# Attention value products of a vision tower: one product for both heads of a step in place of one for each

## The chip, the cores and the metric

The kernel runs on one core of one Trainium2 chip. The metric is the device time of one execution, in microseconds (us). Five engines matter: PE (matrix products, with its weight loads PEld shown apart), ACT, DVE and POOL (elementwise work), and SP, which here only issues transfers. ACT and POOL issue transfers too.

## The reference

64 images become 196 patches and a class token each (197 tokens, 192 features). One causal self-attention layer with 12 heads of 16 features follows, then a layernorm, then a top-2 expert layer with 8 experts and a second layernorm.

```python
q, k, v = jnp.split(x @ w_attn + b_attn, 3, axis=-1)     # 12 heads of 16
att = jnp.einsum('bhqd,bhkd->bhqk', q, k) * (1.0 / math.sqrt(HS))
att = jax.nn.softmax(jnp.where(causal, att, -jnp.inf), axis=-1)
y = jnp.einsum('bhqk,bhkd->bhqd', att, v)
y = y.transpose(0, 2, 1, 3).reshape(Bx, Tx, Cx) @ w_proj + b_proj
```

The change touches the last einsum and how its result reaches the projection.

## The kernel before, in words

The attention part works on pairs of images (32 pairs) in a software pipeline of 36 bodies; each full body works on several pairs at once, in different stages. A body has 12 steps, and a step handles two heads (one pair `j` of heads) of one image. All engines run the same list of steps, and the order on each is written out by hand; the engines meet at semaphores only. Each engine takes its instructions in order, so an instruction that waits holds up all that follow it.

In step s, in this order:

- PE makes turned scores `ST` (keys on the rows) for the step 9 steps back (`turned_first` L634, `turned_second` L640), the scores `S` that give the row maxima (L646, L652, with masks at L658 and L659), and the value products for the step 11 steps back into the one bank `Y` (`values`, L668 and L672). Behind these stand the pieces of the table `PIECES`: `QK` (L589), `V` (L745 to L749), `PR`, the projection (L759), `MX`, the turning of maxima (L724), and the embedding `EB` (L601) of the next pair.
- ACT copies `Y` to `ysb` (L490) in every third step (2, 5, 8, 11), then takes the exponential of `ST` into `p32` (L495, L497), then in steps 0, 3, 6, 9 issues the transfer `rb <- rd` (L507), and then drains what the pieces made (`qk_hi` L521, `nm` L527 with a transfer of its own L531, `vp` and `hres` L545 and L549, `pay` L563, `x_hi` L466).
- DVE reduces `S` to maxima (L841, L844), in steps 2, 5, 8, 11 multiplies `y = ysb * rb` (L852) for the group before and then takes the reciprocal `rd` of the sums (L861), and drains pieces.
- POOL masks `p32` (L430, L434) and splits `x` (L412).

`ST` has one buffer: its next product waits for the exponential of the last. `Y` has one buffer: three steps (six heads) add up in it, and the first value product of a group waits for `ysb` of the group before (semaphore `s_yc`).

The layout of `Y` before: each head has 102 value columns in `vp`, 96 for the features of a group of six heads, zero but for its own 16, and six for the sums of probabilities, one of them ones. So each head's product goes to the same 102 rows and 198 query columns, and adds only to its own rows. A step needs four products: the first 128 keys (198 queries) and the last 70 keys (70 queries) of either head. `p32`, `vp` and `Y` are plain float32, and the compiler makes two PE instructions of each such product. The sums stand on rows 96 to 101 of `Y`; their reciprocals are spread over the 96 feature rows by the transfer `rb <- rd`.

```python
if opens: first_keys(*heads[0], True, False)
for hh, h in heads: last_keys(hh, h)
if not opens: first_keys(*heads[0], False, False)
first_keys(*heads[1], False, j % 3 == 2).then_inc(s_pv, 1)
```

Of the kernel before, what the change touches and what calls it, by code (L numbers as in the profile page):

```python
# [33 lines left out]
P = 128  # L34
# [35 lines left out]
VW1 = CH + NH // 2  # L70
KV = 2 * NH * VW1
# [129 lines left out]
def attention_block(nc, d, shared):  # L201
    with ExitStack() as ctx:
# [9 lines left out]
        wp, wpt = sb("wp", [CH + 1, 2, CX], F32), sb("wp_turned", [CH, 2, C], F32)  # L212
# [3 lines left out]
        bqk, bv = sb("bqk", [P, 3], F32), sb("bv", [CH, 2], F32)  # L216
        bvs = sb("bv_columns", [CH, 2, P], F32)
# [27 lines left out]
        rd, rb = sb("rd", [P, 2, TI], F32), sb("rb", [CH, 2, TI], F32)  # L245
        y = [sb(f"y{n}", [CH + 1, 2, TI], F32) for n in range(2)]
# [56 lines left out]
        def body_at(i):  # L303
            return Banks(i, stages_of(i) if isinstance(i, int) else ALL, full, drained)

# [152 lines left out]
        def _(act):  # L458
            act.dma_start(wp[0:CH, :, E:], d["wp"]).then_inc(s_w, 16)
# [19 lines left out]
            def body(i, turn, par, stages):  # L479
                g = body_at(i)  # L480
                for s in range(STEPS):
                    m = (i - 1) * STEPS + (s - LAG)
                    if s % 3 == 2 and is_step((i - 1) * STEPS + (s - 1) - LAG_PV):

                        im, j, back = value_step(s - 1)
                        grp = j // 3
                        u = (i - back) * 4 + (im * 2 + grp)
                        wait(act, s_ym, u - 1)
                        act.wait_ge(s_pv, (i - 1) * STEPS + (s - LAG_PV))
                        act.activation(ysb[0:VW1, grp, :], Y[0:VW1, 0:TI], ACT.Copy).then_inc(s_yc, 1)  # L490
# [23 lines left out]
                    for name in g.pieces(s):  # L514
# [18 lines left out]
                        elif name[0] == "V":  # L533
                            t = int(name[1])
                            im, hf, _, rows = TILES[t]
                            g.wait_full(act, name)
                            if t < 2:
                                wait(act, s_pv, (i - 2) * STEPS + 6)
                            else:
                                wait(act, s_pv, (i - 2) * STEPS + 12)  # L540
                            if isinstance(i, int) and i == 1:
                                act.wait_ge(s_vset, 4)
                            dst = bass.AP(vp[im], hf * NH * VW1,
                                          [[KV, rows], [6 * VW1, 2], [VW1 + HD, 6], [1, HD]])
                            act.activation(dst, src[0:rows, 0:C].rearrange("p (g h e) -> p g h e", g=2, h=6),  # L545
                                           ACT.Copy).then_inc(s_vc, 1)
# [38 lines left out]
        def _(pe):  # L585
# [30 lines left out]
            for h in range(2):  # L616
                for f in range(2):
                    mm = pe.matmul(G[1][0:CH, h * E:(h + 1) * E], wpt[:, f, h * CH:(h + 1) * CH], wgc[:, f, :],
                                   start=(f == 0), stop=(f == 1))
# [3 lines left out]
            for f in range(2):  # L623
                pe.matmul(G[1][:, 0:CX], bvs[:, f, :], wp[0:CH, f, :], start=(f == 0), stop=False)
# [36 lines left out]
            def values(im, j, b):  # L661

                heads = [(hh, 2 * j + hh) for hh in range(2)]
                opens = j % 3 == 0

                def first_keys(hh, h, start, stop):
                    v0 = vp[im][:, h * VW1:(h + 1) * VW1]
                    return pe.matmul(Y[0:VW1, 0:TI], v0, p32[b][:, hh, 0:TI], start=start, stop=stop)  # L668

                def last_keys(hh, h):  # L670
                    v1 = vp[im][0:T1, (NH + h) * VW1:(NH + h + 1) * VW1]
                    pe.matmul(Y[0:VW1, P:TI], v1, p32[b][0:T1, hh, TI:TI + T1], start=False, stop=False)  # L672

                if opens:
                    first_keys(*heads[0], True, False)
                for hh, h in heads:
                    last_keys(hh, h)
                if not opens:
                    first_keys(*heads[0], False, False)
                first_keys(*heads[1], False, j % 3 == 2).then_inc(s_pv, 1)  # L680

            def body(i, turn, par, stages):
                g = body_at(i)
                for s in range(STEPS):
# [23 lines left out]
                    if is_step(n - LAG_PV):  # L708
# [4 lines left out]
                        if j == 0:  # L713
                            pe.wait_ge(s_vset, 4)
                            pe.wait_ge(s_vc, (i - back) * 4 + (2 * im + 2))
                        pe.wait_ge(s_mask, m * 2 + 2)
                        values(im, j, (s + 1) % 3)
                    for name in g.pieces(s):
# [32 lines left out]
                        elif name[:2] == "PR":  # L751
# [3 lines left out]
                            for hf in range(2):  # L755
                                rows, col = T1 if hf else P, hf * P
                                for f in range(2):
                                    feat = slice(0, CH + 1 - f)
                                    mm = pe.matmul(G[b][0:rows, hf * CX:(hf + 1) * CX],  # L759
                                                   y[im][feat, f, col:col + rows], wp[feat, f, :],  # L760
                                                   start=(f == 0), stop=(f == 1))
# [18 lines left out]
        def _(dve):  # L780
# [11 lines left out]
            for n in range(2):  # L792
                dve.memset(y[n][CH:CH + 1, 0, :], 1.0).then_inc(s_qset, 1)
# [7 lines left out]
            dve.tensor_copy(bvs[:], bv[:].unsqueeze(2).broadcast_to([CH, 2, P])).then_inc(s_const, 1)  # L801
# [8 lines left out]
            dve.tensor_copy(wp[0:CH, :, 0:E], G[1][0:CH, 0:2 * E].rearrange("p (a b) -> p a b", a=2))\  # L810
# [6 lines left out]
            dve.tensor_tensor(wp[CH:CH + 1, 0, :], G[1][CH:CH + 1, 0:CX], bp[CH:CH + 1], ALU.add).then_inc(s_const, 1)  # L817
# [7 lines left out]
            def body(i, turn, par, stages):  # L825
# [4 lines left out]
                for s in range(STEPS):  # L830
# [16 lines left out]
                    if s % 3 == 2 and is_step(n - LAG_PV - 4):  # L847
# [3 lines left out]
                        dve.wait_ge(s_rb[grp], ((i - back) * 2 + (im + 1)) * 16)  # L851
                        dve.tensor_tensor(y[im][0:CH, grp, :], ysb[0:CH, grp, :], rb[:, grp, :],  # L852
                                          ALU.mult).then_inc(s_ym, 1)
                    if s % 3 == 2 and is_step(n - LAG_PV - 1):
# [6 lines left out]
                        dve.reciprocal(rd[CH:VW1, grp, :], ysb[CH:VW1, grp, :])\  # L861
# [117 lines left out]
                    if isinstance(i, int) and i == 0 and s == 6:  # L979
# [5 lines left out]
                        for n in range(2):  # L985
                            dve.memset(bass.AP(vp[n], CH, [[KV, P], [6 * VW1, 4], [VW1 + 1, 6]]), 1.0)\
                                .then_inc(s_vset, 1)
# [554 lines left out]
```

## Time and profile before

| | |
|---|---|
| median of 3 runs | 2326.57 us (2326.23 to 2331.97) |
| the profiled execution: its time | 2324.15 us |
| its span in the trace | 2322.4 us |
| TensorE clock granted, mean | 0.968 of full speed |
| busy over the span | PE 92%, PEld 89%, DVE 68%, POOL 68%, ACT 47% |
| instructions | 49007, of them PE 14772 |

The attention part fills the first 1,300 us or so, the expert part the rest. A row of a timeline gives the start in us, the duration, the engine, the line, the operation, the tile written, the tiles read and the shapes; in brackets stands how long the engine was idle before it and who released it. Matmuls overlap: the next one starts in the trace before the last one ends, so a product's price on PE is the distance from start to start. A row of ACTq is ACT's sequencer issuing a transfer.

### The profile page before, as it was taken

Reading aid. Unit: us, or ns where it says so; the run is one execution under the profiler, and the core shown is the slowest. Engines: PE = TensorE matmul, PEld = TensorE weight load, DVE = VectorE, ACT = ScalarE, POOL = GpSimd, SP = SyncE. Lnnn points to the kernel's source line nnn. Section 1 sums busy time; section 2 is a strip of 40 time slices with the busy share of each in tenths; the row PEclk is TensorE's granted clock in tenths of the full one; section 3 lists DMA queues with packets and bytes.
Section 4 is the critical chain, followed back from the end, with each engine's and each line's share of the span. In section 5 each row is a group of like instructions: output and inputs, shape, how many; then the busy total and the mean of one; then the engine's idle time right before and its main releaser. Section 6 shows DMA issues by size and latency. Waiting matters only on the chain. (4 is left out here: it accounts for less than half of the span.)

```text
span 2322.4 us, 49007 instructions
## 1 busy us (share of the span) xinstructions
PE 2134.6 (92%) x14772; PEld 2068.0 (89%) x14772; DVE 1578.2 (68%) x4286; ACT 1084.3 (47%) x2850; POOL 1577.8 (68%) x2317
## 2 busy tenths in 40 slices
PE   5999999999999999999999479999999999999980
PEld 5999999999999999999988379999999999999980
DVE  5577777777777777777777446666666666665656
ACT  2444444444444444444444245454545445454545
POOL 3366767676767676767656657777777777777756
PEclk8999999999999999999999689999999999999995
DMA  7656565656565656565644143201010101001338
GB/s 204 144 132 146 132 145 130 145 129 145 129 145 130 142 130 142 128 144 128 144 97 99 32 107 56 42 5 29 4 31 5 30 5 29 4 4 24 56 44 334
DMA packets 235842, 223.54 MB, mean 96 GB/s; under 512 B 90647, under 2 KB 216066, under 8 KB 234688
## 3 DMA queue, kind: packets, MB, share of 16 engines
q1 hardware_dynamic: 135872, 147.40, 25.0%
q10 hardware_dynamic: 45568, 59.31, 11.2%
q0 software_dynamic: 54272, 15.20, 5.4%
q8 instruction: 68, 1.11, 0.2%
q14 instruction: 62, 0.51, 0.1%
HBM read 154.56 MB, written 98.38 MB: 109 GB/s over the span
## 5 line engine op out<-in xcount | busy, mean ns | idle before, releaser
L1159 POOL DMA_INDIRECT x_tokens<-yout,e_entry x240 | 383.6, 1598 | 182.5 <-DVE yout L1340 136.1
L668 PE MATMUL Y<-p,vp 128*102 128x198 f32 x1536 | 360.9, 344 | 14.8 <-ACT ysb L490 8.8
L1355 DVE TENSOR_TENSOR a<-UP,gate 128x384 f32<-128x384 f32 x320 | 178.5, 558 | 220.2 <-ACT gate L1295 214.7
L446 POOL DMA_INDIRECT expert_lists<-entry,slot x256 | 290.3, 1134 | 54.1 <-issue 54.1
L495 ACT ACTIVATE p<-ST 128x396 f32<-128x396 f32 x384 | 190.9, 497 | 261.3 <-PE ST L640 254.8
L1144 POOL DMA_INDIRECT rows<-x_wide,e_entry x240 | 249.5, 1040 | 78.8 <-issue 71.9
L1295 ACT ACTIVATE gate<-GT 128x384 f32<-128x384 f32 x320 | 157.8, 493 | 298.2 <-PE UP L1237 298.2
L141 POOL TENSOR_TENSOR word_p<-word_p 1x1 f32<-1x1 f32 x416 | 89.1, 214 | 294.0 <-ACT p L497 282.1
L412 POOL TENSOR_TENSOR x_lo<-x,x_hi 128x396 fp32r<-128x396 f32 x192 | 205.4, 1072 | 80.9 <-ACT x_hi L466 79.2
L668 PEld LDWEIGHTS Y<-p,vp 128*102 128x102 f32 x1536 | 221.7, 170 | 29.6 <-issue 8.8
L841 DVE TENSOR_REDUCE rm<-S 128x2 f32<-128x256 f32 x384 | 161.8, 421 | 106.5 <-PE S L659 104.0
L844 DVE TENSOR_REDUCE rm<-S 70x2 f32<-70x396 f32 x384 | 213.4, 556 | 0.0
L646 PE MATMUL S<-k,q 96*128 96x128 f32 x768 | 184.6, 241 | 17.6 <-DVE rm L844 15.8
L672 PE MATMUL Y<-p,vp 70*102 70x70 f32 x1536 | 191.7, 247 | 1.7 <-POOL p L434 1.7
L672 PEld LDWEIGHTS Y<-p,vp 70*102 70x102 f32 x1536 | 185.5, 171 | 2.7 <-POOL p L434 2.3
L861 DVE RECIPROCAL rd<-ysb 6x198 f32<-6x198 f32 x128 | 177.4, 1386 | 4.7 <-ACT ysb L490 0.8
L1345 DVE TENSOR_TENSOR a_lo<-a,a_hi 128x384 fp32r<-128x384 f32 x320 | 178.2, 560 | 0.0
L1284 ACT ACTIVATE ylo<-Y,e_entry 128x192 f32<-128x192 f32 x240 | 101.2, 422 | 159.7 <-PE Y L1250 159.7
L646 PEld LDWEIGHTS S<-k,q 96*128 96x128 f32 x768 | 147.1, 192 | 31.8 <-DVE rm L844 24.9
L1340 DVE SCALAR_TENSOR_TENSOR yout<-Y,e_entry,ylo 128x192 f32<-128x192 f32 x240 | 100.3, 418 | 109.8 <-ACT ylo L1284 109.5
L430 POOL TENSOR_SCALAR_AFFINE_SELECT p<-p 128x256 f32<-128x256 f32 x384 | 170.5, 444 | 0.0
L652 PE MATMUL S<-k,q 96*70 96x198 f32 x768 | 166.5, 259 | 0.0
(212 smaller groups left out, 6640.8 us busy)
## 6 DMA issues: line engine op xcount, KB each, us to landing
x<-in_xt ACTq DMA_DIRECT2D x180, 198.0 KB
q<-qk_features SPq DMA_DIRECT2D x384, 74.2 KB
k<-qk_features SPq DMA_DIRECT2D x192, 148.5 KB
qk_features<-qk_hi SPq DMA_DIRECT2D x96, 198.0 KB, 2.8
qk_features<-qk_lo SPq DMA_DIRECT2D x96, 198.0 KB, 3.8
rb<-rd ACTq DMA_DIRECT2D x128, 74.2 KB
t_x<-x_tokens SPq DMA_DIRECT2D x15, 576.0 KB, 8.2
out<-t_o ACTq DMA_DIRECT2D x15, 576.0 KB, 8.2
```

The lines of the kernel that those rows point to most:

```text
L412: pool.tensor_tensor(x_lo[:, t], x[:, t], x_hi[:, t].bitcast(F32), ALU.subtract)\
L446: pool.indirect_dma_start(d["lists"][:, :], bass.IndirectOffsetOnAxis(ap=slot[o][0:REAL[t], t, c:c + 1], axis=0), entry[o][0:REAL[t], t, c ...
L495: act.activation(p32[b][:, :, 0:TI], ST[0][:, 0:TP].rearrange("p (h c) -> p h c", h=2), ACT.Exp, scale=SCALE)
L646: pe.matmul(S[0][:, b * P:(b + 1) * P], qt[rows, im, b, j, 0:P], kt[rows, im, j, 0:P], start=(b == 0), stop=False)
L668: return pe.matmul(Y[0:VW1, 0:TI], v0, p32[b][:, hh, 0:TI], start=start, stop=stop)
L672: pe.matmul(Y[0:VW1, P:TI], v1, p32[b][0:T1, hh, TI:TI + T1], start=False, stop=False)
L844: dve.tensor_reduce(rm[im][0:T1, 1, j:j + 7:6], S[1][0:T1, 0:TP].rearrange("p (h c) -> p h c", h=2), AX.X, ALU.max, negate=True).then_inc( ...
L861: dve.reciprocal(rd[CH:VW1, grp, :], ysb[CH:VW1, grp, :])\
L1144: pool.indirect_dma_start(rows[cc % 2][:, t, :], None, d["xin"][:, :], row_of(cc, t), bounds_check=N - 1, oob_is_err=False).then_inc(s_row ...
L1159: pool.indirect_dma_start(d["x1"][:, :], row_of(cc, t), yout[q][:], None, bounds_check=N - 1, oob_is_err=False, compute_op=ALU.add)\
L1345: dve.tensor_tensor(a_lo[cc % 2][:, m], a32[m % 2][:], a_hi[cc % 2][:, m].bitcast(F32), ALU.subtract).then_inc(s_alo, 1)
L1355: dve.tensor_tensor(a32[m % 2][:], UP[m % 2][:, 0:TILE3], gate[m % 2][:], ALU.mult)\
```

## The change

Both heads of a step now share one product. The stationary side holds the value columns of both: 116 of them, in two halves that begin at rows 0 and 64 of the result. In each half row 0 is empty, the next three are the sums of three heads, then 48 feature rows of three heads. The moving side streams the probabilities of both heads, 2 x 198 columns, and the result is 116 x 396. Rows of the lower half are right for the first head's columns alone, rows from 64 on for the second head's columns alone; the other quarters are made and not read. So `values` issues two products in place of four: one over the first 128 keys with 396 columns and one over the last 70 keys with 140 columns. The group of three steps stays.

ACT takes each half from its own columns, in two instructions in place of one, and each with a bias from a column of the identity that puts a one on the empty row. `rb` is filled by two transfers of 48 rows in place of one of 96. The reciprocal now covers rows 0 to 67, the multiplication 116 rows, and the projection's weights are laid out to match (its bias comes from row 0). Four more small fills run once at the start.

```diff
-                        act.activation(ysb[0:VW1, grp, :], Y[0:VW1, 0:TI], ACT.Copy).then_inc(s_yc, 1)
+                        act.activation(ysb[0:V0 + GH * HD, grp, :], Y[0:V0 + GH * HD, 0:TI], ACT.Identity,
+                                       bias=ident[0:V0 + GH * HD, 0:1])
+                        act.activation(ysb[OB:VM, grp, :], Y[OB:VM, TI:TP], ACT.Identity,
+                                       bias=ident[OB:VM, OB:OB + 1]).then_inc(s_yc, 1)
...
-                        src = rd[CH:VW1, grp, :].unsqueeze(1).broadcast_to([NH // 2, HD, TI])
-                        act.dma_start(rb[:, grp, :], src).then_inc(s_rb[grp], 16)
+                        for at in (0, OB):
+                            src = rd[at + 1:at + V0, grp, :].unsqueeze(1).broadcast_to([GH, HD, TI])
+                            act.dma_start(rb[at + V0:at + V0 + GH * HD, grp, :], src).then_inc(s_rb[grp], 16)
...
-                if opens:
-                    first_keys(*heads[0], True, False)
-                for hh, h in heads:
-                    last_keys(hh, h)
-                if not opens:
-                    first_keys(*heads[0], False, False)
-                first_keys(*heads[1], False, j % 3 == 2).then_inc(s_pv, 1)
+                both = Y[0:VM, 0:TP].rearrange("p (h c) -> p h c", h=2)
+                pe.matmul(both, value_columns(im, 0, j), p32[b][:, :, 0:TI], start=(j % GH == 0), stop=False)
+                pe.matmul(both[:, :, P:TI], value_columns(im, 1, j), p32[b][0:T1, :, TI:TI + T1],
+                          start=False, stop=(j % GH == GH - 1)).then_inc(s_pv, 1)
...
-                        dve.wait_ge(s_rb[grp], ((i - back) * 2 + (im + 1)) * 16)
-                        dve.tensor_tensor(y[im][0:CH, grp, :], ysb[0:CH, grp, :], rb[:, grp, :],
+                        dve.wait_ge(s_rb[grp], ((i - back) * 2 + (im + 1)) * 32)
+                        dve.tensor_tensor(y[im][:, grp, :], ysb[0:VM, grp, :], rb[:, grp, :],
                                           ALU.mult).then_inc(s_ym, 1)
...
-                        dve.reciprocal(rd[CH:VW1, grp, :], ysb[CH:VW1, grp, :])\
+                        dve.reciprocal(rd[0:OB + V0, grp, :], ysb[0:OB + V0, grp, :])\
```

PE in step 8, the value products between the masks of the scores and the piece V1. Before:

```order
1501 L659 MATMUL S<-masks 128x256
1504 L668 MATMUL Y<-p_0,vp 102x198
1505 L672 MATMUL Y<-p_0,vp 102x70 x2
1506 L668 MATMUL Y<-p_0,vp 102x198
1507 L745 MATMUL G<-wa_hi,h_hi 70x392
```

And now:

```order
1546 L672 MATMUL S<-masks 128x256
1550 L677 MATMUL Y<-p_0,vp 116x396
1551 L678 MATMUL Y<-p_0,vp 116x2x70
1552 L744 MATMUL G<-wa_hi,h_hi 70x392
```

Four products became two, with as many columns in all; they stand at the same place.

ACT from step 6 on: the transfer `rb <- rd`, the drain of the maxima with its transfer, and what follows up to the copy of `Y` in step 8. Before:

```order
382 L507 DMA rb<-rd 96x1x198
384 L527 ACTIVATE nm<-G 12x198
385 L531 DMA q<-nm 1x12x198
388 L563 ACTIVATE pay<-r,shift,rstd 128x192 x2
393 L495 ACTIVATE p_1<-ST 128x2x198
397 L545 ACTIVATE vp<-G 128x2x6x16
399 L549 ACTIVATE hres<-G 128x200
400 L563 ACTIVATE pay<-r,shift,rstd 128x192 x2
404 L490 ACTIVATE ysb<-Y 102x198
405 L495 ACTIVATE p_2<-ST 128x2x198
```

And now:

```order
400 L521 DMA rb<-rd 48x1x198 x2
402 L541 ACTIVATE nm<-G 12x198
403 L545 DMA q<-nm 1x12x198
406 L576 ACTIVATE pay<-r,shift,rstd 128x192 x2
411 L508 ACTIVATE p_1<-ST 128x2x198
415 L558 ACTIVATE vp<-G 128x6x2x16
417 L562 ACTIVATE hres<-G 128x200
418 L576 ACTIVATE pay<-r,shift,rstd 128x192 x2
422 L500 ACTIVATE ysb<-Y,ident 52x198
423 L502 ACTIVATE ysb<-Y,ident 52x198
424 L508 ACTIVATE p_2<-ST 128x2x198
```

One transfer more stands at the head of this stretch, and one activation more at its end.

## Rows read from the trace of the kernel before

**Rows 1.** Busy time by engine, one full stretch of the attention part.

```profile
600.00:800.00 200.00, 195.45 (x1471) 186.71 (x1472) 153.56 (x483) 96.02 (x282) 139.73 (x275) 1.00 0.60 136
```

**Rows 2.** The page's costliest groups: the value products on PE.

```profile
L668 PE MATMUL Y<-p,vp 128*102 128x198 f32 x1536 | 360.9, 344 | 14.8 <-ACT ysb L490 8.8
...
L672 PE MATMUL Y<-p,vp 70*102 70x70 f32 x1536 | 191.7, 247 | 1.7 <-POOL p L434 1.7
```

**Rows 3.** Timeline of PE, the value products of one step (step 9).

```profile
801.68 0.49 PE L672 MATMUL Y<-p,vp 70*102 70x70 f32 x4
802.01 0.86 PE L668 MATMUL Y<-p,vp 128*102 128x198 f32 x4
802.71 1.53 PE L759 MATMUL G<-wp,y 97*128 97x200 f32 x8
```

**Rows 4.** Timeline of ACT, steps 0 to 2 of a body, and the next body's step 0.

```profile
813.15 0.50 ACT L495 ACTIVATE p<-ST 128x396 f32<-128x396 f32 x1 [0.92 <-PE ST L640]
813.27 0.77 ACTq L507 DMA_DIRECT2D rb<-rd  x1
...
814.17 0.53 ACT L513 ACTIVATE h_hi<-ht 128x396 fp32r<-128x396 f32 x1 [0.34 <-issue]
...
815.38 0.79 ACTq L531 DMA_DIRECT2D q<-nm  x1
816.36 0.54 ACT L466 ACTIVATE x_hi<-x 128x396 fp32r<-128x396 f32 x1 [1.02 <-issue]
816.80 0.49 ACT L495 ACTIVATE p<-ST 128x396 f32<-128x396 f32 x1
...
817.47 0.59 ACT L521 ACTIVATE qk_hi<-G,bqk 128x396 fp32r<-128x396 f32 x1
817.96 0.52 ACT L466 ACTIVATE x_hi<-x 128x396 fp32r<-128x396 f32 x1
818.38 0.33 ACT L490 ACTIVATE ysb<-Y 102x198 f32<-102x198 f32 x1
818.60 0.50 ACT L495 ACTIVATE p<-ST 128x396 f32<-128x396 f32 x1
...
852.04 0.50 ACT L495 ACTIVATE p<-ST 128x396 f32<-128x396 f32 x1 [0.92 <-PE ST L640]
```

**Rows 5.** Timeline of PE in step 2.

```profile
817.51 0.45 PE L634 MATMUL ST<-q,k 97*128 97x396 f32 x1
...
818.26 0.27 PE L659 MATMUL S<-masks 128*128 128x256 bf16 x1
818.84 0.58 PE L668 MATMUL Y<-p,vp 128*102 128x198 f32 x2 [0.31 <-POOL p L434]
```

**Rows 6.** Timeline of DVE, steps 5 and 6.

```profile
829.82 0.43 DVE L841 TENSOR_REDUCE rm<-S 128x2 f32<-128x256 f32 x1 [0.59 <-PE S L659]
...
831.02 1.39 DVE L861 RECIPROCAL rd<-ysb 6x198 f32<-6x198 f32 x1
...
832.78 0.56 DVE L844 TENSOR_REDUCE rm<-S 70x2 f32<-70x396 f32 x1
```

**Rows 7.** Timeline of ACT, steps 6 to 8.

```profile
832.44 0.79 ACTq L507 DMA_DIRECT2D rb<-rd  x1
833.43 0.33 ACT L527 ACTIVATE nm<-G 12x198 fp32r<-12x198 f32 x1 [1.55 <-PE G L725]
...
837.55 0.33 ACT L490 ACTIVATE ysb<-Y 102x198 f32<-102x198 f32 x1
```

**Rows 8.** Timeline of PE in steps 7 and 8.

```profile
833.39 0.33 PE L646 MATMUL S<-k,q 96*128 96x128 f32 x1 [0.35 <-DVE rm L844]
...
837.58 0.27 PE L659 MATMUL S<-masks 128*128 128x256 bf16 x1
838.01 0.58 PE L668 MATMUL Y<-p,vp 128*102 128x198 f32 x2 [0.15 <-ACT ysb L490]
```

**Rows 9.** Timeline of ACT: the shortest issue of a transfer on its queue.

```profile
821.27 0.34 ACTq L575 DMA_DIRECT2D x<-in_xt  x1
```

**Rows 10.** ACT's issue and DVE's wait for its landing, in the last bodies.

```profile
1275.15 0.79 ACTq L507 DMA_DIRECT2D rb<-rd  x1
...
1279.31 0.36 DVE L852 TENSOR_TENSOR y<-ysb,rb 96x198 f32<-96x198 f32 x1 [4.20 <-DMA rb<-rd]
```

More of the change, by code:

```diff
@@ L69 @@
 REAL = [T - P if hf else P for _, hf, _, _ in TILES]
-VW1 = CH + NH // 2
-KV = 2 * NH * VW1
+OB, GH = 64, NH // 4
+V0 = 1 + GH
+VM = OB + V0 + GH * HD
+VSTEP = VM + HD
+KV = 2 * WA
 ROWS_QK = 3 * 2 * HD
@@ L215, in attention_block @@
         bps = sb("bp_wide", [CH, 2, P], F32)
[L216 to L217 removed]
+        bqk, bv = sb("bqk", [P, 3], F32), sb("bv", [VM, 2], F32)
+        bvs = sb("bv_columns", [VM, 2, P], F32)
         bp = sb("bp", [P, CX], F32)
@@ L244, in attention_block @@
         ysb = sb("ysb", [P, 2, TI], F32)
-        rd, rb = sb("rd", [P, 2, TI], F32), sb("rb", [CH, 2, TI], F32)
-        y = [sb(f"y{n}", [CH + 1, 2, TI], F32) for n in range(2)]
+        rd, rb = sb("rd", [P, 2, TI], F32), sb("rb", [VM, 2, TI], F32)
+        y = [sb(f"y{n}", [VM, 2, TI], F32) for n in range(2)]
         r = sb("r", [P, 4, CX], F32)
@@ L304, in body_at, with value_columns @@
             return Banks(i, stages_of(i) if isinstance(i, int) else ALL, full, drained)
+        HALF = 2 * GH * VSTEP
+        def value_columns(im, hf, j):
+            at = hf * HALF + j // GH * (GH * VSTEP) + j % GH * VM
+            return vp[im][0:T1 if hf else P, at:at + VM]
         def score_step(s):
@@ L541, in body @@
                             if isinstance(i, int) and i == 1:
[L542 to L545, printed above, removed]
+                                act.wait_ge(s_vset, 6)
+                            dst = bass.AP(vp[im], hf * HALF + V0, [[KV, rows], [VSTEP, 6], [OB, 2], [1, HD]])
+                            act.activation(dst, src[0:rows, 0:C].rearrange("p (j b e) -> p j b e", j=6, b=2),
                                            ACT.Copy).then_inc(s_vc, 1)
@@ L623, in _ @@
             for f in range(2):
-                pe.matmul(G[1][:, 0:CX], bvs[:, f, :], wp[0:CH, f, :], start=(f == 0), stop=False)
+                pe.matmul(G[1][:, 0:CX], bvs[:, f, :], wp[:, f, :], start=(f == 0), stop=False)
             for f in range(2):
@@ L757, in body @@
                                 for f in range(2):
-                                    feat = slice(0, CH + 1 - f)
                                     mm = pe.matmul(G[b][0:rows, hf * CX:(hf + 1) * CX],
-                                                   y[im][feat, f, col:col + rows], wp[feat, f, :],
+                                                   y[im][:, f, col:col + rows], wp[:, f, :],
                                                    start=(f == 0), stop=(f == 1))
@@ L791, in _ @@
             dve.memset(q[0][:].bitcast(F32), 0.0).then_inc(s_qset, 1)
-            for n in range(2):
-                dve.memset(y[n][CH:CH + 1, 0, :], 1.0).then_inc(s_qset, 1)
+            for t in (ysb, rb):
+                dve.memset(t[:], 1.0).then_inc(s_qset, 1)
             dve.wait_ge(s_whi, 1)
@@ L985, in body @@
                         for n in range(2):
-                            dve.memset(bass.AP(vp[n], CH, [[KV, P], [6 * VW1, 4], [VW1 + 1, 6]]), 1.0)\
-                                .then_inc(s_vset, 1)
+                            for hf in range(2):
+                                dve.memset(bass.AP(vp[n], hf * HALF + 1, [[KV, P], [GH * VSTEP, 2], [VM + 1, GH],
+                                                                          [OB, 2]]), 1.0).then_inc(s_vset, 1)
                     if s == 8 and "E" in stages:
@@ L1487, in halves, with y_rows @@
         return w.reshape(2, CH, -1).transpose(1, 0, 2)
+    def y_rows(w):
+        full = np.zeros((VM, 2) + w.shape[1:], f32)
+        for b in range(2):
+            at = OB * b + V0
+            full[at:at + GH * HD] = w.reshape((2, GH, 2, HD) + w.shape[1:])[:, :, b].swapaxes(0, 1)\
+                .reshape((GH, 2, HD) + w.shape[1:]).swapaxes(1, 2).reshape((GH * HD, 2) + w.shape[1:])
+        return full
     by_row = np.arange(C).reshape(NH // 2, 2 * HD).T.ravel()
```

28 lines of the change are left out of this document (10 added, 18 removed).

## The prediction

> **What bounds the kernel now.** I began with the busy times by stretch. In the attention part PE is busy 195.45 of 200 us at full clock, ACT only 96.02 [rows 1]. So PE seems to be the bound and ACT seems to have half its time to spare. The page's groups then say what the value products are on PE: two groups of 1536 instructions, and before the larger one 14.8 us of idle time, 8.8 of them put down to the copy of `Y` on ACT [rows 2]. That second figure is the one to follow. The chain of waits that ended last runs through the expert part and says nothing of this one, so I read the timelines of one body instead. A body lasts 852.04 - 813.15 = 38.89 us, from step 0's exponential to the next body's [rows 4].
>
> In the timeline of ACT the reader is to see that its idle half is not spread evenly. In steps 0 to 2 it runs without a gap of its own making: the issue of `rb <- rd` from 813.27 to 814.04, then at 814.17 the first split of `ht`; the issue of `q <- nm` from 815.38 to 816.17, then `x_hi` at 816.36 ("1.02 <-issue"); and from there instruction upon instruction up to the copy of `Y` at 818.38 [rows 4]. An issue of a transfer holds ACT's next instruction, for 0.77 to 0.79 us here. PE follows this chain. Its `ST` of step 2 starts at 817.51, just as ACT is done with the exponential of step 1 (begun at 816.80, next instruction at 817.47), and its first value product starts at 818.84, 0.13 us after `ysb` ends (818.38 + 0.33), though its last product before was at 818.26 [rows 4, 5]. The row names POOL as releaser, but the copy of `Y` is what ended last.
>
> Steps 6 to 8 are the same: `rb <- rd` is issued at 832.44, as the reciprocal ends (831.02 + 1.39 = 832.41), `nm` follows at 833.43, and so on to `ysb` at 837.55; PE's value product starts at 838.01, 0.13 us after it, with the products before it at 837.58 [rows 6 to 8]. And in between DVE decides once: `S` of step 7 starts at 833.39 as DVE's reductions end (832.78 + 0.56 = 833.34), with an idle of 0.35 us before it [rows 6, 8].
>
> **The change part by part.**
>
> *PE's products.* Start to start, four instructions of 70 columns take 802.01 - 801.68 = 0.33 us, 0.0825 each, and four of 198 columns take 802.71 - 802.01 = 0.70 us, 0.175 each: 1.03 us a step [rows 3]. At the granted clock of 1.00 [rows 1], which is 2.4 GHz, 198 columns at two cycles each are 0.165 us, so a long instruction costs its columns and 0.01 us, and a short one (70 columns are 0.058 us) 0.024 us more. Now there are two of 396 columns, 2 x (0.33 + 0.01) = 0.68, and two of 140 columns, 2 x (0.117 + 0.013) = 0.26: 0.94 us. That saves **0.09 us a step**. Bounds: a straight line through both points (0.033 us and 0.00072 a column) gives 0.90 us, a saving of 0.13; prices in proportion to the columns give 1.03, no saving. I take 0.09, since it takes the columns at the rate of the clock. Over 384 steps this would be 35 us if nothing but PE counted.
>
> *The copy of Y.* One copy of 102 x 198 took 0.33 us and the next activation started 0.22 us after it (818.38 to 818.60) [rows 4]. Now there are two, each with a bias from a column. `qk_hi` has such a bias and takes 0.59 for 396 columns where the exponential takes 0.50, so a bias is 0.09 [rows 4]: the first copy passes on after 0.31 us and the second ends 0.42 after that. `ysb` is complete **0.40 us** later than before after the same start. Bounds: 0.22 (no price for the bias) and 0.51.
>
> *The second transfer.* One more issue in steps 0, 3, 6 and 9. Issues of transfers inside the core take 0.77 (96 rows) and 0.79 (12 rows), without regard to their rows [rows 4], so 48 rows should take the same: **0.79 us** more of ACT's sequencer. Lower bound 0.34, the load of `x` from memory [rows 9]; upper bound 0.85.
>
> *Where this lands.* Steps 0 to 2: all of ACT's chain behind the issue moves by 0.79 us, so `ST` of step 2 starts 0.79 later, and the first value product 0.79 + 0.40 = 1.19, say **1.2 us** later. Nothing eats this up, since both were already waited for by PE [rows 4, 5]. Steps 6 to 8: the same, **1.2 us**, counted from the end of the reciprocal [rows 6 to 8]. Steps 3 to 5: ACT's second issue in step 3 ends before `ST` of step 4 is there, and the later `ysb` in step 5 costs PE some 0.13 us, but the next thing PE waits for is DVE's chain from step 5's scores through the reciprocal (829.82 to 833.34), which does not depend on it [rows 6]. Covered, and if DVE had no such chain it would cost 0.13 a body. Steps 9 to 11: ACT is idle before the exponentials there (0.92 us before that of step 0 [rows 4]); the second copy fits in. Covered.
>
> *How much of PE's saving counts.* The savings of steps 0 and 1 fall under ACT's chain, that of step 7 too, and those of steps 5 and 6 under DVE's. Seven steps are left (2, 3, 4 and 8 to 11): 7 x 0.09 = 0.63 us a body. Net: 2 x 1.2 - 0.63 = **1.8 us a body lost**.
>
> *The sum.* The chain of steps 0 to 2 is complete in some 28 bodies (those with value products behind and an embedding ahead), that of steps 6 to 8 in 30 (those with `pay`): 28 x 1.2 + 30 x 1.2 = 70 us. Savings: 30 x 0.63 = 19 us. The last three bodies have little PE work and run by latencies: about six group ends with 0.4 to 0.8 us each, and the last `y` behind two issues, 4 us. The fills at the start: under 1 us. The reciprocal over 68 rows and the product over 116 have the same columns, so nothing. Together 70 - 19 + 4 = +55 us on the profiled execution's own 2324.15 us (span 2322.4): 2379 us. The median of the runs is 2.4 us higher, so I give 2381 us for the new median. In the expert part nothing changes.
>
> *The landing of rb.* `y = ysb * rb` waits for it. Issue end to `y` was 1279.31 - 1275.94 = 3.4 us where nothing else delayed it [rows 10]. In steps 6 to 8 the new second issue ends at 834.03 and `y` comes at 839.1 or so, once DVE has done step 8's scores, 5 us later. In steps 0 to 2 it is 5 to 6 us. So the landing stays hidden by 1.6 us, if two transfers take no longer than one.
>
> The section "Why a DMA increments its semaphore by 16 and not by 1" of the page "DMA: Bandwidth & Descriptors" of the Trainium skill has a rule against this: a transfer from these queues uses as many of the 16 engines as divide the outermost dimension of both sides. That would make 6 of the old transfer (6 source rows) and 3 of each new one, the same three both times by the same section. No row here shows it.
>
> **The rivals.**
>
> *A. The forecast, slower by the ACT chain*: 2381 us. For it: two places in every body where PE starts 0.13 us after `ysb`. Against it: nothing I found; its size hangs on the price of the second issue. With 0.34 us in place of 0.79 the sum is 58 x (0.34 + 0.40) - 19 + 3 = +27 us, 2353 us; with 0.13 us saved a step 9 us less.
>
> *B. Faster: ACT's added work is hidden and PE's saving is not.* This is the reading of the busy shares, ACT at 48% [rows 1]. Its place is the head of steps 2 and 8. It needs the second issue to cost ACT's next instruction nothing (say because the sequencer overlaps it), and the copies to fit into PE's present slack. Then 384 x 0.09 = 35 us less, 2292 us. It decides in that direction as soon as the added delay at each place is below 7 x 0.09 / 2 = 0.32 us. Against it: 0.13 us gaps at both places, and `h_hi` starting 0.13 us behind the issue.
>
> *C. Slower still: rb lands late.* If each new transfer runs on half the engines and they share them, the transfer's own part of the 3.4 us doubles or more, to some 5 to 6 us, and `y` in steps 2 and 8, with the reciprocal behind it and the maxima behind that, waits up to 1 us each. For steps 6 to 8 this enters the chain above. Some +30 us more: 2411 us. Against it: in all the full bodies DVE never waits for `rb`.
>
> *D. The merge saves PE nothing*, because the price goes by columns: 19 us more than A, 2400 us.
>
> **How the numbers follow.** A with its sizes 0.62, D 0.08, C 0.13, B 0.10, and 0.07 that the places recover part of the delay and leave it within 0.3% (7 us, which is about what a measurement of this kernel can tell from no change). A, C and D are slower. The range must reach over A's bounds (2346 to 2395) and to C: 2343 to 2413 us. Left out are B and the near tie. Faster by over 0.3%: 0.10, within: 0.07, slower: 0.83.
>
> **What would show it.** PE's instructions fall by 1536 to 13236. A value step takes 0.94 us start to start. In ACT's timeline two issues of `rb <- rd` of about 0.79 us stand in a row before `h_hi` (step 0) and before `nm` (step 6), and the first value product of steps 2 and 8 begins 0.13 us behind the second copy. PE's idle time charged to `ysb` (or to POOL's mask in its place) before `Y` grows from 14.8 to some 60 us or more, with more before `ST`. A body takes 40.7 us in place of 38.89. I would be wrong if the second issue is short or overlapped, if DVE waits for `rb` in full bodies, or if a value step takes 1.03 us still.

## The result and the profile after

The changed kernel takes 2383.7 us (2378.65 to 2386.07, 4 runs) against 2326.4 us before: a ratio of 1.0246, with an interval of 1.0211 to 1.0281. It is slower by 57 us; the forecast was 2381. The profiled execution took 2378.65 us with a span of 2376.9. Of all executions below, one of b_two_columns ran at a mean granted clock of 0.555 and took 3524.66 us; its ratio leaves it out.

The page's group of the long value products and the stretch 600 to 800 us of the changed kernel, to be set beside [rows 1, 2]:

```profile
L677 PE MATMUL Y<-p,vp 128*116 128x396 f32 x768 | 334.1, 517 | 62.0 <-ACT ysb L502 60.5
```

```profile
600.00:800.00 200.00, 183.26 (x1157) 153.24 (x1157) 145.19 (x439) 101.27 (x284) 130.18 (x261) 0.99 0.54 130
```

PE is busy 183 us of 200 in place of 195, and its idle time before the value products went from 14.8 to 62.0 us, 60.5 of it put down to the second copy of `Y` (L502). ACT is still only half busy. The page counts 13236 PE instructions, 1536 fewer, as the diff says.

The value products of one step on PE, beside [rows 3]:

```profile
817.73 0.83 PE L677 MATMUL Y<-p,vp 128*116 128x396 f32 x2
818.40 0.40 PE L678 MATMUL Y<-p,vp 70*116 70x140 f32 x2
818.64 1.52 PE L757 MATMUL G<-wp,y 116*128 116x200 f32 x8
```

Start to start it is 0.67 us for the two long ones and 0.24 for the two short ones, 0.91 us in place of 1.03. So the merging itself saves 0.12 us a step.

ACT in steps 0 to 2, beside [rows 4]:

```profile
808.17 0.50 ACT L508 ACTIVATE p<-ST 128x396 f32<-128x396 f32 x1 [0.91 <-PE ST L653]
808.30 0.76 ACTq L521 DMA_DIRECT2D rb<-rd  x1
...
809.10 0.73 ACTq L521 DMA_DIRECT2D rb<-rd  x1
810.02 0.53 ACT L527 ACTIVATE h_hi<-ht 128x396 fp32r<-128x396 f32 x1 [1.18 <-issue]
...
813.20 0.58 ACT L535 ACTIVATE qk_hi<-G,bqk 128x396 fp32r<-128x396 f32 x1
813.67 0.53 ACT L476 ACTIVATE x_hi<-x 128x396 fp32r<-128x396 f32 x1
814.10 0.41 ACT L500 ACTIVATE ysb<-Y,ident 52x198 f32<-52x198 f32 x1
814.53 0.42 ACT L502 ACTIVATE ysb<-Y,ident 52x198 f32<-52x198 f32 x1
814.97 0.50 ACT L508 ACTIVATE p<-ST 128x396 f32<-128x396 f32 x1
...
850.58 0.53 ACT L527 ACTIVATE h_hi<-ht 128x396 fp32r<-128x396 f32 x1 [1.08 <-issue]
```

And PE in step 2, beside [rows 5]:

```profile
813.36 0.45 PE L647 MATMUL ST<-q,k 97*128 97x396 f32 x1 [0.31 <-ACT p L510]
...
814.11 0.27 PE L672 MATMUL S<-masks 128*128 128x256 bf16 x1
815.08 0.92 PE L677 MATMUL Y<-p,vp 128*116 128x396 f32 x2 [0.70 <-ACT ysb L502]
```

Two issues stand ahead of `h_hi`, 0.80 us apart. From step 0's exponential to step 2's value product it was 818.84 - 813.15 = 5.69 us [rows 4, 5] and is 815.08 - 808.17 = 6.91: 1.22 us more. PE still starts 0.13 us behind the copy (814.53 + 0.42 = 814.95). The reader should note that the two copies do not overlap: 0.43 us from start to start at a length of 0.41. Nor does the exponential overlap the second copy (814.97 against 814.95). The body lasts 850.58 - 810.02 = 40.56 us.

The second issue and the copies should have made 0.80 + 0.52 = 1.32 us, and 0.10 of it is missing. It went where `qk_hi` starts. These are the last product that `qk_hi` drains and the activation ahead of it, before:

```profile
817.09 0.34 PE L589 MATMUL G<-h,wa_lo 128*128 128x396 f32 x1
817.19 0.27 ACT L497 ACTIVATE p<-ST 70x140 f32<-70x140 f32 x1
```

And now:

```profile
812.70 0.34 PE L602 MATMUL G<-h,wa_lo 128*128 128x396 f32 x1
813.03 0.27 ACT L510 ACTIVATE p<-ST 70x140 f32<-70x140 f32 x1
```

Before, PE's product ended at 817.43 and `qk_hi` started at 817.47 [rows 4], when the exponential had ended (817.46). Now PE is done at 813.04 and `qk_hi` starts at 813.20, 0.10 us ahead of the exponential's end, as back-to-back activations from row 0 do in these traces. So in the body of [rows 4] PE's own work was 0.1 us later than ACT's chain. In the kernel before `qk_hi` starts 3.19 and 3.30 us behind `h_hi` in turn from one full body to the next; in the changed kernel it is 3.18 to 3.20 in every full body.

Steps 5 to 8 of DVE, ACT and PE, beside [rows 6 to 8]:

```profile
825.69 0.43 DVE L839 TENSOR_REDUCE rm<-S 128x2 f32<-128x256 f32 x1 [0.60 <-PE S L672]
...
826.97 1.38 DVE L859 RECIPROCAL rd<-ysb 68x198 f32<-68x198 f32 x1
```

```profile
828.38 1.54 ACTq L521 DMA_DIRECT2D rb<-rd  x2
830.11 0.33 ACT L541 ACTIVATE nm<-G 12x198 fp32r<-12x198 f32 x1 [2.11 <-issue]
...
834.24 0.42 ACT L500 ACTIVATE ysb<-Y,ident 52x198 f32<-52x198 f32 x1
834.67 0.42 ACT L502 ACTIVATE ysb<-Y,ident 52x198 f32<-52x198 f32 x1
```

```profile
825.82 0.92 PE L677 MATMUL Y<-p,vp 128*116 128x396 f32 x2 [0.16 <-ACT ysb L502]
...
835.23 0.92 PE L677 MATMUL Y<-p,vp 128*116 128x396 f32 x2 [1.11 <-ACT ysb L502]
```

From the reciprocal's end to the value product of step 8 it was 838.01 - 832.41 = 5.60 us and is 835.23 - 828.35 = 6.88: 1.28 us more. The wait of 0.16 us in step 5 costs nothing: from step 5's first maximum to the reciprocal's end it is 2.66 us, and was 2.59.

The transfers of `rb` over the full bodies 600 to 1200 us, in the view of its tile:

```profile
L521 ACTq DMA_DIRECT2D rb<-rd x118: 734/747/789, 603.4 to 1198.3; - x118
L850 DVE TENSOR_TENSOR y<-ysb,rb x59: 349/351/565, 600.9 to 1195.7; 116x198 f32<-116x198 f32 x59
```

An issue takes 0.75 us in the median, and the view lists nobody who waited for `rb`.

One thing here the prediction did not have. Between the first splits `h_hi` of 29 bodies lie 28 intervals; 22 of the changed kernel's are 39.5 to 40.9 us (mostly 40.5 to 40.8), and five are 42.2 to 42.4 (the last is 42.5 in either kernel). In those five, and nowhere else between 120 and 1195 us, PE's granted clock fell to 0.50 for about 3 us behind the wait of step 8. The two rows are the same 2 us, counted from the value product of step 8, of such a body and of its neighbour:

```profile
711.60:713.60 2.00, 1.92 (x5) 1.24 (x5) 1.90 (x3) 0.65 (x2) 0.79 (x3) 0.52 1.07 261
671.00:673.00 2.00, 1.98 (x12) 1.60 (x13) 1.84 (x3) 0.66 (x3) 0.79 (x3) 1.00 1.06 271
```

```profile
711.68 1.66 PE L677 MATMUL Y<-p,vp 128*116 128x396 f32 x2 [1.11 <-ACT ysb L502]
```

The granted clock is 0.52 there, near the 1.2 GHz level, and five matmuls begin in the time of twelve. The wait ahead was the same 1.11 us in both bodies. Each such body lost some 1.6 us, 8 us together. The kernel before, which waits there for 0.15 to 0.18 us in most bodies and not at all in the others, shows one such stretch, in its last full body (from 1182 us).

### The profile page after: what moved, and what is told of

Same layout as the page of the kernel before. It is cut to its first block and busy times, and to the rows that moved or that the text cites. A ratio compares the mean times of both kernels' runs of the same rounds, so it can differ in the third digit from the quotient of the medians.

```text
span 2376.9 us, 46193 instructions
## 1 busy us (share of the span) xinstructions
PE 2117.3 (89%) x13236; PEld 1911.3 (80%) x13236; DVE 1574.5 (66%) x4288; ACT 1157.3 (49%) x2978; POOL 1557.4 (66%) x2317
## 5 line engine op out<-in xcount | busy, mean ns | idle before, releaser
L677 PE MATMUL Y<-p,vp 128*116 128x396 f32 x768 | 334.1, 517 | 62.0 <-ACT ysb L502 60.5
L456 POOL DMA_INDIRECT expert_lists<-entry,slot x256 | 284.0, 1109 | 54.2 <-issue 54.2
L144 POOL TENSOR_TENSOR word_p<-word_p 1x1 f32<-1x1 f32 x416 | 78.5, 189 | 334.2 <-ACT p L510 327.6
L678 PEld LDWEIGHTS Y<-p,vp 70*116 70x116 f32 x768 | 140.7, 183 | 121.6 <-issue 121.6
L677 PEld LDWEIGHTS Y<-p,vp 128*116 128x116 f32 x768 | 110.8, 180 | 85.6 <-issue 41.8
L859 DVE RECIPROCAL rd<-ysb 68x198 f32<-68x198 f32 x128 | 176.5, 1379 | 3.2 <-issue 2.5
L647 PE MATMUL ST<-q,k 97*128 97x396 f32 x384 | 149.9, 390 | 23.4 <-ACT p L510 23.0
```

Source lines behind the costliest of these rows:

```text
L456: pool.indirect_dma_start(d["lists"][:, :], bass.IndirectOffsetOnAxis(ap=slot[o][0:REAL[t], t, c:c + 1], axis=0), entry[o][0:REAL[t], t, c ...
L677: pe.matmul(both, value_columns(im, 0, j), p32[b][:, :, 0:TI], start=(j % GH == 0), stop=False)
```

## The experiments

Theory 1 is the prediction's: ACT's chain in steps 0 to 2 and 6 to 8 took the loss. Theory 2 puts it on the late landing of `rb`, theory 3 on the merged products. All times are medians, and ratios are against the kernel before. Its median was 2324.42 us over the first 7 executions, 2324.88 over 13 and 2322.71 over 17; differences are taken from the one of the same group of experiments.

### Each part alone

**b_two_issues.** In the kernel before:

```diff
-                        src = rd[CH:VW1, grp, :].unsqueeze(1).broadcast_to([NH // 2, HD, TI])
-                        act.dma_start(rb[:, grp, :], src).then_inc(s_rb[grp], 16)
+                        for at in (0, 3):
+                            src = rd[CH + at:CH + at + 3, grp, :].unsqueeze(1).broadcast_to([3, HD, TI])
+                            act.dma_start(rb[at * HD:(at + 3) * HD, grp, :], src).then_inc(s_rb[grp], 16)
```

> The kernel before, with rb filled by two transfers of 48 rows in place of one of 96; products and copy as before. Theory 1 (the ACT chain of steps 0 to 2 and 6 to 8): each further issue of 0.75 to 0.79 us moves the first value product of steps 2 and 8 in some 58 places, 58 x 0.77 = 45 us and 2 us at the end: about 2373 us, and no wait of DVE for rb in the full bodies. Theory 2 (the landing of rb is what hurts): the time grows too, but DVE's multiplication waits for rb in full bodies. Theory 3 (the merged products themselves cost time, ACT is hidden): 2326 us, no change.

Measured: 2370.96 us, ratio 1.0192 (1.0170 to 1.0215), 46.5 us slower. The tile view has the same issue time and nobody waiting for `rb`:

```profile
L508 ACTq DMA_DIRECT2D rb<-rd x119: 734/747/1624, 603.6 to 1199.7; - x119
L853 DVE TENSOR_TENSOR y<-ysb,rb x60: 350/351/353, 601.2 to 1197.4; 96x198 f32<-96x198 f32 x60
```

So one more issue costs nearly what ACT's sequencer spends on it, at two places in a body, and nothing waits for the data. The typical body is 40.3 us, 1.4 more, or 0.70 for each place. The 28 intervals make 39.4 of the 46.9 us between the profiled executions and 7.4 lie outside them, where 45 and 2 were expected, so that the total agrees better than its parts. Theory 3 does not explain this, since nothing was merged, and theory 2 is out.

**b_two_copies.** The copy of `Y` in the kernel before, as two:

```diff
-                        act.activation(ysb[0:VW1, grp, :], Y[0:VW1, 0:TI], ACT.Copy).then_inc(s_yc, 1)
+                        act.activation(ysb[0:64, grp, :], Y[0:64, 0:TI], ACT.Identity,
+                                       bias=ident[0:64, 127:128])
+                        act.activation(ysb[64:VW1, grp, :], Y[64:VW1, 0:TI], ACT.Identity,
+                                       bias=ident[64:VW1, 127:128]).then_inc(s_yc, 1)
```

> The kernel before, with Y copied by two biased activations (rows 0 to 63 and 64 to 101, same columns, bias zero) in place of one plain copy. Theory 1: ysb is complete 0.52 us later (0.43 from copy to copy and 0.42 for the second, against 0.33), 58 x 0.52 = 30 us: about 2357 us. Theory 2 and theory 3: nothing or under 5 us.

Measured: 2363.39 us, 1.0162 (1.0141 to 1.0184), 39 us slower. The typical body grew from 38.8 to 39.0 us to 39.9 to 40.07, 1.08 us, which is 2 x 0.52 and makes the 30 us that were expected. Of the rest, 4 us lie in the last interval of the full bodies (46.6 us in place of 42.5), 0.8 ahead of the first, and the others behind the last, where the pipeline drains. Their cause was not looked into.

**m_lower_half.** The merged products, with the copy and the transfer as before in number:

```diff
-                        act.activation(ysb[0:V0 + GH * HD, grp, :], Y[0:V0 + GH * HD, 0:TI], ACT.Identity,
-                                       bias=ident[0:V0 + GH * HD, 0:1])
-                        act.activation(ysb[OB:VM, grp, :], Y[OB:VM, TI:TP], ACT.Identity,
-                                       bias=ident[OB:VM, OB:OB + 1]).then_inc(s_yc, 1)
+                        act.activation(ysb[0:VM, grp, :], Y[0:VM, 0:TI], ACT.Copy).then_inc(s_yc, 1)
...
-                        for at in (0, OB):
-                            src = rd[at + 1:at + V0, grp, :].unsqueeze(1).broadcast_to([GH, HD, TI])
-                            act.dma_start(rb[at + V0:at + V0 + GH * HD, grp, :], src).then_inc(s_rb[grp], 16)
+                        src = rd[1:V0, grp, :].unsqueeze(1).broadcast_to([GH, HD, TI])
+                        act.dma_start(rb[V0:V0 + GH * HD, grp, :], src).then_inc(s_rb[grp], 16)
```

> The merged products, but Y copied by one plain copy of 116 rows from the first head's columns, and rb filled by one transfer of 48 rows: the second head of each step is not handed on rightly (its rows are read from the wrong columns, and not normalised), so this leaves a part of the computation out and shows what PE's saving is worth alone. Theory 1: a value step is 0.12 us shorter, and in 7 of 12 steps that counts, 7 x 0.12 x 30 = 25 us: 2301 us. If all 12 steps counted: 46 us, 2281 us. Theory 3 (merged products cost time): 2326 us or above.

Measured: 2290.94 us, 0.9851 (0.9832 to 0.9870), 33.5 us faster, where 25 were expected. The body takes 38.0 us, 0.9 less, for which 7 x 0.12 = 0.84 was expected; all twelve steps would have given 1.44. `qk_hi` starts 3.18 to 3.20 us behind `h_hi` in every full body here, which gives back 0.11 in every other one. The 28 intervals make 26.4 us and 7.1 lie outside them; why, was not looked into. Theory 3 is out: the merged products are the gain, and some seven steps of it count.

The three parts alone add up to 46.5 + 39.0 - 33.5 = 52 us, of the 57 measured together. In the 28 intervals between full bodies they fit closely: 39.4 + 32.9 - 26.4 = 45.9 us, against 53.4 in the changed kernel, of which 8 come from the lower clock. Outside them the parts make 7.4 + 6.6 - 7.1 = 6.9 us and the changed kernel 1.1. That difference stays open.

### The issue on another queue

**m_rb_sp** and **b_rb_sp.** In the changed kernel and in the kernel before, SP issues `rb <- rd` in steps 0, 3 and 6:

```diff
+                    if s in (0, 3, 6) and is_step((i - 1) * STEPS + (s - 2) - LAG_PV):
+                        im, j, back = value_step(s - 2)
+                        grp = j // 3
+                        u = (i - back) * 4 + (im * 2 + grp)
+                        sp.wait_ge(s_rd, u + 1)
...
```

> The changed kernel, with the two transfers of rb issued from SP in steps 0, 3 and 6 (in step 9 ACT keeps them). Theory 1: ACT's chain loses both issues, 1.5 us at both places, but keeps the two copies: against the kernel before 0.25 us to 0.4 less at step 2 and about 0.1 more at step 8, with PE's 0.84 us a body: about 2290 us, some 90 us below the changed kernel. Theory 2: DVE would still wait for the two transfers; under 30 us below the changed kernel. Theory 3: no difference from the changed kernel, 2384 us.

> The kernel before with the transfer of rb issued from SP in steps 0, 3 and 6; nothing merged. The control for m_rb_sp: theory 1 says that the place of the issue is worth something by itself, about 0.4 us at both places: 58 x 0.4 = 23 us, about 2302 us, so that the merged kernel with the issues on SP (2313 us) still stands behind it by what its two copies cost over what PE saves. If the gain of m_rb_sp came from the merging, this would stay at 2325 us.

Measured: m_rb_sp 2312.91 us, 0.9946 (0.9927 to 0.9966), 71 us below the changed kernel (8 of them because no stretch at the lower clock is left in its full bodies); b_rb_sp 2320.42 us, 0.9978 (0.9968 to 0.9988), 4.5 us below the kernel before (2.3 below the median over all 17 of its executions). The direction held in both, but both sizes were too hopeful, by 23 and 18 us. ACT's timeline of b_rb_sp from step 0's exponential on shows why:

```profile
810.85 0.50 ACT L502 ACTIVATE p<-ST 128x396 f32<-128x396 f32 x1 [0.92 <-PE ST L647]
...
811.42 0.53 ACT L520 ACTIVATE h_hi<-ht 128x396 fp32r<-128x396 f32 x1
...
815.17 0.59 ACT L528 ACTIVATE qk_hi<-G,bqk 128x396 fp32r<-128x396 f32 x1 [0.33 <-PE G L596]
```

`h_hi` begins 0.57 us after the exponential in place of 1.02, but `qk_hi` now waits 0.33 us for PE and begins 815.17 - 810.85 = 4.32 us after it, exactly as before (817.47 - 813.15 [rows 4]). Step 8 is the same: `nm` starts 0.53 us behind the reciprocal's end in place of 1.02, but the copy of `Y` 5.05 us behind it in place of 5.14. In the kernel before, PE's own work was within 0.1 us of ACT's chain at both places, so taking work from ACT gave hardly anything. Adding to it cost nearly the full price.

### The copies

**m_plain_copies** and **m_rb_sp_plain** make the two copies plain ones in the changed kernel and in m_rb_sp:

```diff
-                        act.activation(ysb[0:V0 + GH * HD, grp, :], Y[0:V0 + GH * HD, 0:TI], ACT.Identity,
-                                       bias=ident[0:V0 + GH * HD, 0:1])
-                        act.activation(ysb[OB:VM, grp, :], Y[OB:VM, TI:TP], ACT.Identity,
-                                       bias=ident[OB:VM, OB:OB + 1]).then_inc(s_yc, 1)
+                        act.activation(ysb[0:V0 + GH * HD, grp, :], Y[0:V0 + GH * HD, 0:TI], ACT.Copy)
+                        act.activation(ysb[OB:VM, grp, :], Y[OB:VM, TI:TP], ACT.Copy).then_inc(s_yc, 1)
```

> The changed kernel with its two copies of Y as plain copies, without the bias that puts a one on the empty rows, so the projection's bias and its part of the gate's input are left out. Theory 1: if the bias is what makes a copy 0.42 us and keeps the next from overlapping it, ysb is complete 0.55 us after the start in place of 0.85, 58 x 0.30 = 17 us less than the changed kernel: about 2366 us. If two copies from one bank don't overlap for another reason (0.33 and 0.33), 58 x 0.19 = 11 us less, 2372 us. Theory 2 and 3: no change from 2384 us.

> m_rb_sp with plain copies as in m_plain_copies (the projection's bias left out). Theory 1: 58 x 0.30 = 17 us below m_rb_sp: about 2296 us.

Measured: 2370.83 us, 1.0201 (1.0184 to 1.0219), 13 us below the changed kernel; and 2303.33 us, 0.9905 (0.9888 to 0.9922), 10 us below m_rb_sp, where 17 were expected. That is the second of the two cases for the first kernel and its price (11 us) for the other. The profiled execution of m_plain_copies also has six full bodies with a stretch at the granted clock of 0.5 behind the wait of step 8 (0.91 to 0.93 us there), about as many as the changed kernel, so that these do not make the difference. ACT's timeline of m_plain_copies:

```profile
797.77 0.32 ACT L500 ACTIVATE ysb<-Y 52x198 f32<-52x198 f32 x1
798.10 0.33 ACT L501 ACTIVATE ysb<-Y 52x198 f32<-52x198 f32 x1
```

Start to start 0.33, as long as one lasts, so the bias is 0.09 us of each copy and the missing overlap has another cause.

**b_two_columns.** The kernel before with `Y` copied in two plain activations on the same rows, columns 0 to 98 and 99 to 197:

```diff
+                        act.activation(ysb[0:VW1, grp, 0:TI // 2], Y[0:VW1, 0:TI // 2], ACT.Copy)
+                        act.activation(ysb[0:VW1, grp, TI // 2:TI], Y[0:VW1, TI // 2:TI], ACT.Copy).then_inc(s_yc, 1)
```

> The kernel before with Y copied in two plain activations that share the rows and split the columns (99 and 99). Two activations on rows 0 to 51 and 64 to 115 followed each other without any overlap, where others overlap by 0.1 us. If it is the start row that forbids the overlap, the two here start 0.14 us apart and ysb is 0.06 us later: 58 x 0.06 = 3 us, 2328 us. If two copies of one bank into one tile never overlap, 0.25 and 0.25: 0.17 us later, 10 us, 2335 us.

```profile
801.63 0.24 ACT L490 ACTIVATE ysb<-Y 102x99 f32<-102x99 f32 x1
801.76 0.25 ACT L491 ACTIVATE ysb<-Y 102x99 f32<-102x99 f32 x1
```

In the trace these two overlap: 0.13 us from start to start at a length of 0.24. So two copies out of one bank can overlap. That the rows are others is not enough to forbid it: the exponentials of 128 and then 70 rows overlap by 0.10 us in every kernel here. The activations that did not overlap are those from row 64 on, with the one ahead of them and with the exponential from row 0 behind them, although its 128 rows include theirs. So what is left is the first row; whether it is row 64 itself or the change of the first row was not separated. The time was 2332.12 us, 1.0034 (1.0020 to 1.0047), 9 us more and not 3. The bodies account for 3 (0.12 us each), and the last interval of the full bodies for another 3 (45.8 us in place of 42.5), so the median alone would have pointed to the wrong case.

**m_rb_sp_split.** In m_rb_sp, DVE copies the upper half (`tensor_scalar`, at the head of steps 2, 5, 8 and 11) while ACT copies the lower.

> m_rb_sp with the upper half of Y copied by DVE at the head of the step while ACT copies the lower half. Complete result. Theory 1: ysb is complete 0.43 us earlier at steps 2 and 8, 58 x 0.43 = 25 us below m_rb_sp less what 0.3 us more on DVE costs in step 5's chain (nothing if DVE is idle there, 0.59 us before): about 2288 us, below the kernel before. If DVE's chain binds instead, 2300 us or more, with longer waits of S on the maxima.

Measured: 2334.15 us, 1.0035 (1.0020 to 1.0049), 21 us above m_rb_sp, where 25 us below it were expected. DVE and PE in step 2:

```profile
781.88 0.63 DVE L892 SCALAR_TENSOR_TENSOR qk_lo<-G,bqk,qk_hi 128x396 fp32r<-128x396 f32 x1 [1.42 <-ACT qk_hi L542]
782.54 0.43 DVE L844 TENSOR_SCALAR ysb<-Y,ident 52x198 f32<-52x198 f32 x1
```

```profile
783.20 0.92 PE L684 MATMUL Y<-p,vp 128*116 128x396 f32 x2 [0.98 <-DVE ysb L844]
```

DVE's copy stands behind `qk_lo`, which waits for ACT; it ends at 782.97, later than ACT's (782.17 + 0.41), and PE waits for it. Counted from `h_hi`, the upper half is there after 5.22 us, and in m_rb_sp, with both copies on ACT, after 5.12: nothing is gained. I had asked how long the copy takes on DVE and not what it is queued behind. This makes a part of the 21 us only. The body takes some 0.4 us more over 26 intervals, and the last two are 42.5 and 43.3 us in place of 38.5 and 38.2, 9 us together, with a stretch at the lower clock in the second of them; their cause was not looked into.

### Towards a better version

**m_one_row** is complete: m_rb_sp with plain copies. The row of ones stands at row 51, between the copied halves, where one fill at the start reaches it:

```diff
-V0 = 1 + GH
+V0, ONE = GH, GH + GH * HD
...
+            sp.wait_ge(s_const, 5)
+            sp.dma_start(wp[ONE:ONE + 1, 0, :], biasrow[:]).then_inc(s_row, 16)
```

> A complete kernel: merged products, rb issued from SP in steps 0, 3 and 6, and plain copies of Y. The row of ones that carries the projection's bias stands outside the copied rows (row 51, filled once), so no bias is needed in the copy; its weights' row is placed by one transfer at the start. Theory 1: the same order and prices as m_rb_sp_plain, so about 2303 us, some 22 us below the kernel before and 80 below the changed kernel.

**m_one_row_pay** and **b_rb_sp_pay** also move two `pay` activations from ahead of step 8's copy of `Y` to behind its exponential.

> m_one_row with the two later pay activations moved from step 7 behind the exponential of step 8, so 0.88 us less of ACT's work stands ahead of the copy of Y in step 8. Theory 1: PE's wait for ysb at step 8 (0.6 us or less with the plain copies) goes: 30 x 0.4 to 0.6 = 12 to 18 us below m_one_row, about 2288 us. If step 8 is not a place of the chain: 2303 us.

> The same move of pay in b_rb_sp (nothing merged), as the control. Theory 1: with the single copy PE's wait there is 0.3 us or less: at most 30 x 0.3 = 9 us below b_rb_sp, 2311 to 2320 us; the merged kernel m_one_row_pay then leads it by PE's saving, 20 us or more.

Measured: m_one_row 2300.62 us, 0.9892 (0.9873 to 0.9911). m_one_row_pay **2292.42 us, 0.9858 (0.9837 to 0.9880)**, the fastest complete version, 34 us below the median that the study began with, 30 below the kernel before's median over 17 executions, and 91 below the changed kernel. It is 8 us below m_one_row, where 12 to 18 were expected. b_rb_sp_pay 2310.03 us, 0.9931 (0.9909 to 0.9954). Bodies take 38.13, 37.63 and 38.51 us. So step 8 was a place of the chain even in the kernel before (b_rb_sp to b_rb_sp_pay, 10 us, where 9 at most were expected), and once ACT's two places are relieved, the merging, with its two copies, is worth 18 us on equal terms. That is less than the 20 that were expected and under half of what PE saves in all steps (384 x 0.12 = 46).

## Why the prediction was right, point by point

- **What bounds the kernel.** Right for work added to ACT: its chain at the head of steps 2 and 8 sets the pace, and not its busy share. PE starts its value products 0.13 or 0.14 us behind the copy at both places, as forecast. Rival B, which read the busy shares, fell. But the reading that PE only follows ACT there was incomplete: PE's own work was within 0.1 us of the same time, once even later, as `qk_hi` and b_rb_sp show. For an added issue this tie cost the forecast 0.1 us in every other body; for an issue taken away it was nearly everything.
- **PE's products.** Mis-sized: 0.94 us a step was forecast, 0.91 measured, so the saving is 0.12 in place of 0.09. The long products cost 0.335 us each (0.34 forecast) and the short ones 0.12 (0.13 forecast). The straight line through both points, my bound, was nearer (0.90). Rival D fell.
- **The copy of Y.** Mis-sized the other way: 0.40 us later was forecast, 0.52 measured (0.43 and 0.42 against 0.33), just past my bound of 0.51. The price of the bias was right (0.09), but I took for granted that the two copies overlap as others do; only the bound allowed for the other case.
- **The second transfer.** Right: 0.75 us in the median, 0.77 to 0.83 from issue to issue, with 0.79 forecast. The issue of 96 rows is 0.79 in the median, so 48 rows are a little shorter, against the forecast that rows do not matter. b_two_issues alone gave 46.5 us.
- **Where it lands.** 1.2 us was forecast at both places, 1.22 and 1.28 measured. Two slips are in this: the copies took 0.52 in place of 0.40, and of the issue, 0.79 by the forecast, 0.70 and 0.75 were left where the first copy starts (814.10 - 808.17 against 818.38 - 813.15, and 834.24 - 828.35 against 837.55 - 832.41). At the first place the missing 0.10 is PE's lateness at `qk_hi` before. The two slips nearly cancel. Step 5 was covered by DVE's chain, and steps 9 to 11 show no wait for `ysb`, as said.
- **How much of PE's saving counts.** Seven steps of twelve: m_lower_half's body lost 0.9 us, 7.5 steps' worth, and the half step is what `qk_hi` gains in every other body.
- **The body.** 40.7 us was forecast; measured were 40.5 to 40.8, in 28 intervals 53.4 us more than before. In that sum the larger saving of PE (0.21 us a body) and the longer copies (0.24) cancel, and some 8 us come from the lower clock, which no step of mine had.
- **The ends.** 4 us were forecast; beside the 28 intervals only 1.1 us are left (54.5 - 53.4).
- **The landing of rb.** Right, it stays hidden. The rule of the Trainium skill on the engines that a transfer uses (page "DMA: Bandwidth & Descriptors", section "Why a DMA increments its semaphore by 16 and not by 1") had no consequence here: no wait for `rb` in any full body, with two transfers or one. Rival C fell. Whether the rule holds was not seen.

So the total of 2381 against 2383.7 is closer than its terms deserve: the copies were 7 us too cheap over 58 places, PE's saving 6 us too small over 30 bodies, and the 8 us of the lower clock were missing, against 3 us too much for the ends and some 3 us for the issues. On the profiled execution the forecast was 2379 us and 2378.65 were measured. Four executions of the changed kernel spread over 7 us, so a miss of 1 or 3 us says nothing, and the cancelling of these terms was luck. The mechanism does not hang on it: b_two_issues, b_two_copies and m_lower_half show its three terms one by one.

## What to carry to other kernels

Before fewer and larger products are bought with more work on the engine that drains them, read in the timeline where the draining engine runs without gaps, and price every added issue of a transfer there in full, for an engine that is half idle on average can still set the pace at two places. Relief at such a place is worth only the distance to what is late next, while an addition costs nearly all of its time, so the two directions must be worked out apart. And work that moves to another engine is priced by what it queues behind there.

## What was not expected of the hardware

- An activation that starts at row 64 did not overlap the one from row 0 ahead of it (rows 0 to 51, then 64 to 115; or 0 to 63, then 64 to 101): 0.33 us apart at 0.32 for plain ones, 0.43 at 0.41 with a bias. Nor did the exponential from row 0 overlap the one from row 64 ahead of it (0.44 at 0.42). Activations that all start at row 0 overlap by 0.1 us, also with 128 rows and then 70, or 102 and then 128 (0.22 apart at 0.33 [rows 4]); two halves of columns were 0.13 us apart at 0.24.
- Behind a wait of 1.11 us PE's granted clock was 0.52 over the next 2 us in 5 of 28 bodies, and 1.00 in a body whose wait was as long. Each time it cost some 1.6 us. With waits of 0.91 to 0.93 us there m_plain_copies shows it in six full bodies. m_rb_sp and b_two_issues, with 0.58 us, show it in none, and the kernel before, with 0.15 to 0.18, in its last full body alone.
- The issue of a transfer inside the core takes ACT nearly the same time whether it fills 96 rows (0.79 us in the median), 48 (0.75) or 12 (0.80), and back to back two of 48 rows are 0.77 to 0.83 us apart.
